# A transformer block on one Trainium2 core: the first batch's row maxima turned by quarters of the heads, the second's by halves

## The reference

```python
c6 = silu(c) @ Wc + bc            # six modulation vectors for each batch
sh_msa, sc_msa, g_msa, sh_mlp, sc_mlp, g_mlp = split(c6, 6)
xm = layernorm(x) * (1 + sc_msa) + sh_msa
q, k, v = (xm @ W + b).reshape(B, S, NH, DH)  for W, b in (q, k, v)
w = softmax((q / DH) @ k.T)                   # 512 x 512 for each batch and head
x = x + g_msa * ((w @ v) @ Wo + bo)
xm2 = layernorm(x) * (1 + sc_mlp) + sh_mlp
x = x + g_mlp * (gelu(xm2 @ W1 + b1) @ W2 + b2)
```

## Time and profile before

| | |
|---|---|
| Median of 3 runs | 773.78 us (772.47 to 776.5) |
| Profiled execution | 772.2 us |
| Its span in the profile | 770.0 us |
| Mean granted TensorE clock | 0.954 |
| PE busy | 709.4 us (92%) |
| DVE busy | 580.5 us (75%) |
| ACT busy | 391.1 us (51%) |
| POOL busy | 216.5 us (28%) |

### The profile page before, as it was taken

One profiled execution on the slowest core, in us unless ns is written; L12 is line 12 of the kernel. 1 busy time (PEld: TensorE's weight loads), 2 busy tenths in 40 slices (PEclk: granted clock), 3 DMA queues, 4 the chain that ended last, 5 costly groups with the idle time before them and its releaser, 6 DMA issues.

```text
span 770.0 us, 11786 instructions
## 1 busy us (share of the span) xinstructions
PE 709.4 (92%) x3967; PEld 382.9 (50%) x3967; DVE 580.5 (75%) x1019; ACT 391.1 (51%) x463; POOL 216.5 (28%) x162
## 2 busy tenths in 40 slices
PE   4788989869999999999999999999999998998996
PEld 2451222432378325762478225862478225822886
DVE  4779788959896998789886798789886986721563
ACT  5420556127742775257642675257633773298221
POOL 1454020200343032512162032412162022330444
PEclk9875899869999999999999999999999999999999
DMA  8599000771058303850076303840076102021110
GB/s 295 197 262 261 22 29 20 253 170 55 29 194 207 112 15 114 252 147 29 28 239 160 102 14 131 239 143 29 29 239 166 65 27 72 3 83 44 57 35 27
DMA packets 59846, 88.45 MB, mean 115 GB/s; under 512 B 6246, under 2 KB 47740, under 8 KB 56716
## 3 DMA queue, kind: packets, MB, share of 16 engines
q1 hardware_dynamic: 59788, 87.69, 37.0%
HBM read 49.35 MB, written 38.06 MB: 114 GB/s over the span
## 4 chain that ended last, share of the span: by engine, by line
PE 35%; issue 34%; DVE 14%; POOL 11%; ACT 3%; DMA 3%; POOLq 0%; SPq 0%; ACTq 0%; DVEq 0%
DVE mx L947 7%; PE ps L651 7%; PE ps L629 7%; PE ps L574 6%; PE ps L659 5%; POOL hl L462 4%; PE ps L795 4%; PE ps L799 2%; POOL prob L452 2%; ACT prob L520 2%; DVE prob L1019 1%; POOL x L432 1%; POOL xd L445 1%; PE ps L611 1%; PE ps L731 1%
## 5 line engine op out<-in xcount | busy, mean ns | idle before, releaser
L947 DVE TENSOR_REDUCE mx<-ps 128x1 f32<-128x512 f32 x512 | 336.0, 686 | 60.8 <-PE ps L629 54.7
L520 ACT ACTIVATE prob<-ps 128x1024 f32<-128x1024 f32 x256 | 247.8, 1022 | 155.4 <-PE ps L659 155.2
L629 PE MATMUL ps<-kst,qst 96*128 96x512 bf16 x512 | 197.5, 407 | 22.5 <-DVE mx L947 17.1
L659 PE MATMUL ps<-qst,kst 98*128 98x512 bf16 x512 | 150.6, 386 | 4.2 <-DMA qst<-mrow 2.7
L629 PEld LDWEIGHTS ps<-kst,qst 96*128 96x128 bf16 x512 | 45.5, 98 | 189.8 <-DVE mx L947 165.9
L651 PE MATMUL ps<-prob,vaug 128*32 128x512 f32 x1024 | 137.8, 610 | 0.5 <-ACT prob L520 0.3
L462 POOL TENSOR_TENSOR hl<-z,hh 128x512 fp32r<-128x512 f32 x64 | 82.3, 1286 | 136.5 <-DVE hh L1079 136.5
L561 ACT ACTIVATE z<-ps,bias_t 128x512 f32<-128x512 f32 x64 | 44.0, 688 | 134.7 <-PE ps L799 129.9
L409 POOL TENSOR_TENSOR rstd<-vare,mhalf 128x4 f32<-128x4 f32 x16 | 16.7, 1046 | 255.2 <-DVE vare L875 255.2
L659 PEld LDWEIGHTS ps<-qst,kst 98*128 98x128 bf16 x512 | 47.1, 99 | 70.6 <-ACT prob L520 26.9
L452 POOL TENSOR_TENSOR prob<-prob 128x512 bf16<-128x512 f32 x32 | 38.3, 1196 | 139.8 <-DVE prob L1022 139.8
(11 more groups left out here) (106 smaller groups left out, 833.0 us busy)
## 6 DMA issues: line engine op xcount, KB each, us to landing
parts_scratch<-prob SPq DMA_DIRECT2D x32, 384.0 KB, 2.9
qst<-parts_scratch SPq DMA_DIRECT2D x16, 768.0 KB, 9.1
kst<-parts_scratch SPq DMA_DIRECT2D x16, 768.0 KB, 13.6
parts_scratch<-prob SPq DMA_DIRECT2D x32, 256.0 KB, 3.2
y_scratch<-rb SPq DMA_DIRECT2D x32, 256.0 KB, 2.0
xa<-in_x_dram SPq DMA_DIRECT2D x8, 512.0 KB, 4.3
parts_scratch<-prob SPq DMA_DIRECT2D x32, 128.0 KB, 2.9
xd<-in_x_dram SPq DMA_DIRECT2D x8, 512.0 KB, 3.5
```

The source lines that it names most:

```text
L520: act.activation(prob[:, s % 2, 2 * p:2 * p + 2, :], ps[:, 2 * p:2 * p + 2, :], ACT.Exp, scale=1.0 / DH).then_inc(exp_done, 1)
L629: pe.matmul(ps[:, banks[n % len(banks)], :], qst[1 - par][0:MROW, h, t * P:(t + 1) * P], kst[1 - par][0:MROW, h, :], start=True, stop=True ...
L659: m = pe.matmul(ps[:, q, :], kst[par][0:KROWS, G * g + q, kt * P:(kt + 1) * P], qst[par][0:KROWS, G * g + q, :], start=True, stop=True)
L947: dve.tensor_reduce(mx[:, t, h:h + 1], ps[:, banks[n % len(banks)], :], AXX, ALU.max).then_inc(max_done, 1)
```

## The change

Four things are changed.

**Smaller turns.** Batch 0 is turned in four quarters: 18 blocks, the turn of heads 0 to 3, and 6 blocks in step -1; the other 40 in the first ten stages of C(0), with turns at s = 2, 6 and 10. Batch 1 is turned in two halves: 24 blocks in s = 10 to 15 of C(0), 6 in A, 2 behind it, the turn, 12 more; the other 20 in the first six stages of C(1), with a turn at s = 6. So the 64 blocks of batch 2 begin at s = 7 of step 1. From step 2 on the order of blocks is as before.

**The second batch's x** is loaded among the first loads, into `x1`; its statistics wait for that, and its normalisation and the splitting of Wv and Wo stand at another place in VectorE's order.

**Part writes.** Each part has one place in SBUF and is written by one transfer to all its slots, as soon as that part is there. There are as many transfers and bytes as before.

**Waits.** C(0) no longer waits for the low parts of the MLP weights on GpSimd (`const_set`); the products with Wo do.

```diff
-C_BLOCKS = (1, 0) + (3,) * (STEPS - 4) + (4, 4)
-TURN_BLOCKS, QK_BLOCKS, V_BLOCKS = (1, 1), (0, 1, 0, 1), (0, 1, 0, 1)
-UP_BLOCKS, DOWN_BLOCKS = (1, 1, 1), (2, 2, 2, 2, 2, 0, 0, 0)
-HALF, EXTRA = NH * TT // 2, 8
-OLD_BLOCKS = (4,) * 6 + (0,) * (STEPS - 6)
-NEW_BLOCKS = (0,) * 6 + (4,) * (STEPS - 6)
+QUARTER, HALF, EXTRA, SECOND = NH * TT // 4, NH * TT // 2, 8, 44
+Blocks = namedtuple("Blocks", "old new turn qk v up down")
+STEADY = Blocks((0,) * STEPS, (1, 0) + (3,) * (STEPS - 4) + (4, 4), (1, 1), (0, 1, 0, 1), (0, 1, 0, 1), (1, 1, 1), (2, 2, 2, 2, 2, 0, 0, 0))
+FIRST = Blocks((4,) * 10 + (0,) * 6, (0,) * 10 + (4,) * 6, (1, 1), (0, 1, 0, 1), (0, 1, 0, 1), (), ())
+NEXT = Blocks((2, 2, 4, 4, 4, 4) + (0,) * 10, (0,) * 7 + (3, 3) + (4,) * 7, (1, 1), (1,) * 4, (1,) * 4, (2, 2, 2), (3, 3, 3, 3, 2, 0, 0, 0))
+FIRST_TURNS, NEXT_TURNS = {2: 4, 6: 8, 10: 12}, {6: 8}
...
+            sp.dma_start(x1[:], x[1].rearrange("(t p) f -> p t f", p=P)).then_inc(xb_loaded, 16)
...
                 def write_parts(b, j):
-                    sp.wait_ge(part_l, 4 * b + j + 1)
-                    for slot, part, n in SLOT_RUNS[j // 2]:
-                        sp.dma_start(parts_scr[j, slot:slot + n].rearrange("n p s -> p n s"), parts[:, j, part:part + n, :])\
-                            .then_inc(parts_written[j], 16)
+                    for part, ready in enumerate((part_h, part_m, part_l)):
+                        at, step, n = PART_SLOTS[j // 2][part]
+                        sp.wait_ge(ready, 4 * b + j + 1)
+                        sp.dma_start(parts_scr[j, at:at + (n - 1) * step + 1:step].rearrange("n p s -> p n s"),
+                                     parts[:, j, part, :].unsqueeze(1).broadcast_to([P, n, S])).then_inc(parts_written[j], 16)
...
-                        pe.wait_ge(const_set, 6)
+                        pe.wait_ge(const_set, 3)
...
-                        if s == STEPS // 2 and not later(i, 0, 1):
-                            pe.wait_ge(m_loaded, 32)
+                        if s in (4, 8, 12) and at(i, 0) or s == 8 and at(i, 1):
+                            pe.wait_ge(m_loaded, 32 * turn_no(i, s))
...
+                        if turn is not None:
+                            turn_maxima(i, turn)
                         if s:
                             pv(i, par, s - 1)
-                        between(2, old + new)
-                        if s == OLD_TURN and not later(i, 0, 1):
-                            turn_maxima(i - 1, NH // 2, NH)
+                        between(2 if turn is None else 0, old + new)
...
                 elif early(i):
-                    scores(i, par, HALF + 2, (6, 7, 0, 1))
-                    turn_maxima(i, 0, NH // 2, half_turned, 4)
+                    scores(i, par, QUARTER + 2, (6, 7, 0, 1))
+                    turn_maxima(i + 1, 0, 4)
                     scores(i, par, EXTRA - 2)
                 else:
-                    scores(i, par, tail_blocks(i))
-                    turn_maxima(i)
+                    scores(i, par, HALF - block_at[0])
+                    turn_maxima(i + 1, 0)
+                    scores(i, par, SECOND - HALF)
```

More of the change, by code:

```diff
@@ L238, in x1_of, with at, blocks, c_turns @@
             return xa if final(b) else x1
[L240 to L247, removed]
+        def at(b, n):
+            return isinstance(b, int) and b == n
+        def blocks(i):
+            return FIRST if at(i, 0) else NEXT if at(i, 1) else STEADY
+        def c_turns(i):
+            return FIRST_TURNS if at(i, 0) else NEXT_TURNS if at(i, 1) else {}
+        def heads_of(b, head):
+            return head + (NH // 4 if at(b, 0) else NH // 2 if at(b, 1) else NH)
+        def turn_no(b, head):
+            return head // 4 + 1 if at(b, 0) else head // 8 + 5 if at(b, 1) else b + 5
         def early(i):
@@ L290, in step @@
             def step(i, par):
-                if runs(i, 2) and later(i, 2, 1) and not early(i) or early(i) and not later(i, 2, 1):
-                    b = i + 3 if early(i) else i + 2
+                if runs(i, 2) and not early(i):
+                    b = i + 2
                     sp.wait_ge(tp_done[0], b)
@@ L303, in step, with load_maxima @@
                     sp.dma_start(gm[:], c6_scr[bass.ds(i - 1, 1), G2 * H:(G2 + 1) * H].broadcast_to([P, H])).then_inc(gm_loaded, 16)
-                def load_maxima(stack, first, last, loaded):
+                def load_maxima(b, stack, head):
+                    last = heads_of(b, head)
+                    sp.wait_ge(mrow_done, 2 * turn_no(b, head))
                     for n in range(2):
-                        sp.dma_start(stack[MROW + n:MROW + n + 1, first:last, :], mrow[0:last - first, n, :]).then_inc(loaded, 16)
-                if runs(i, 0) and not later(i, 0, 1):
-                    sp.wait_ge(mrow_done, 2)
-                    load_maxima(qst[par], NH // 2, NH, m_loaded)
+                        sp.dma_start(stack[MROW + n:MROW + n + 1, head:last, :], mrow[0:last - head, n, :]).then_inc(m_loaded, 16)
                 if runs(i, 0):
+                    if at(i, 0):
+                        load_maxima(i, qst[par], 4)
                     for g in range(NG):
@@ L684, in step @@
                     for s in range(STEPS):
-                        old, new = c_blocks(i, s)
+                        old, new, turn = blocks(i).old[s], blocks(i).new[s], c_turns(i).get(s)
                         def between(first, last):
@@ L755, in step @@
                 else:
-                    scores(i, par, others(sum(QK_BLOCKS + V_BLOCKS)))
+                    scores(i, par, others(sum(blocks(i).qk + blocks(i).v)))
                 def wo_products(bank):
@@ L993, in step @@
                                     norm_piece(0, i + 2, xa, k)
-                    if s == OLD_TURN and has_c and not later(i, 0, 1):
-                        maxima_rows(i - 1, NH // 2)
-                row_max(i, others(TURN_BLOCKS[0]))
+                row_max(i, others(blocks(i).turn[0]))
                 if has_a:
@@ L1024, in step @@
                 for j in range(4):
+                    if j == 2 and has_a and not later(i, 2, 1):
+                        split_weights(1)
+                        for t in range(TT):
+                            normalise(0, 1, x1, t)
                     if j == 3:
-                        row_max(i, others(QK_BLOCKS[3] + sum(V_BLOCKS[0:2])))
+                        row_max(i, others(blocks(i).qk[3] + sum(blocks(i).v[0:2])))
                     if has_a:
```

148 lines of the change are left out of this document (76 added, 72 removed).

## The result

| | before | after |
|---|---|---|
| Median | 774.41 us (772.47 to 776.5, 4 runs) | 787.57 us (785.5 to 788.57, 4 runs) |
| Profiled execution, its span | 772.2, 770.0 us | 785.5, 783.7 us |

The changed kernel is slower: ratio 1.0154, 95% interval 1.0124 to 1.0184. The two spans differ by 13.7 us. Places in the program are read from one profiled execution of each kernel.

A forecast was written before the change was run, and what follows sets the result against it. TensorE (92% busy) and VectorE (75%) were taken to bound the kernel by where each waits. Terms -9.6 + 5.2 + 1.0 + 9.2 + 3.8 + 3.9 = +13.5 us gave 785.7, or 787 by median; predicted 786, range 774 to 792.

The forecast's parts named there:

- start of C(0): Step -1: 16 fewer blocks and an earlier start, but row loads wait behind the load of `qst`; -9.6 us.
- C(0): Same 64 blocks, but three turns at 2.5 us each and 0.6 for statistics, where one cost 2.86; +5.2 us.
- end of step 0: Before C(1): work 1.8 us shorter but worth nothing, because C(1) starts with the stack loads; 0 us.
- first product with v of C(1): Start of C(1): half clock 1.0 us, and blocks ahead waiting for VectorE to write x1, 2.85 us; +3.85 us.
- rest of C(1): C(1) after its first product with v: fuller stages, a turn, a row wait and layernorm pieces; +6.35 us.
- A of step 1: A, up to the MLP's first cast: five more blocks on a full VectorE; +3.8 us (2 to 4.5).
- MLP of step 1: Four times three blocks instead of two, each third waiting for VectorE; +3.9 us (1 to 5).
- the rival that they don't: Step -1: first rows don't wait behind the load of `qst`, C(0) starts at 62.2; 783 us, no separate chance.
- third rival: C(0): a quarter's rows come late, 1 to 2 us in three places; 790 us; late rows or slower clock 0.10.
- the fourth: C(0): turns are cheap and it begins at full clock, -3.2 and -1.6 us; 781 us, no separate chance.
- The wait at s = 8: C(1): rows of the turn at s = 6 land after they are needed; 0.9 us of waiting.
- rivals in which step 1 takes its blocks for nothing or by half: Step 1: blocks free, 769 us (free or nearly so 0.11), or half absorbed, 777 us (774 to 781: 0.17).

The follow-up runs named there:

- experiment 3: Changed kernel with the row loads of step -1 issued ahead of all four stack loads; ratio 1.0124 to the kernel before.
- Experiment 8: Changed kernel with the row loads of steps -1 and 0 issued by ScalarE instead of SyncE; ratio 1.0133 to the kernel before.
- experiment 4: Changed kernel with the row loads of step 0 issued ahead of the four stack loads of step 0; ratio 1.0095 to the kernel before.
- experiment 5: Changed kernel with one block instead of four ahead of C(1)'s first product with v, three more ending step 0; ratio 1.0118 to the kernel before.
- experiment 6: Changed kernel with the third block in step 1's MLP issued behind the next up products, not ahead; ratio 1.0131 to the kernel before.
- experiment 7: Changed kernel with batch 0 in quarters but batch 1 not split, its 34 remaining blocks ending step 0; ratio 1.0019 to the kernel before.
- experiment 10: Changed kernel with rows first in steps -1 and 0, one block ahead of C(1)'s first product with v, third MLP blocks later; ratio 0.9991 to before.
- 11: Kernel before with both start edits and step 0's row loads between the stack loads of heads 0 to 7 and 8 to 15; ratio 0.9891, median 768.06 us.
- 1: Kernel before with the start edits alone: batch 1's x among the first loads, each part written by one transfer; ratio 0.9952 to before.
- 9: Kernel before with step 0's row loads placed between the stack loads of heads 0 to 7 and 8 to 15; ratio 0.9954 to before.

## Why the prediction was right

Sign and time (786 against 787.57 us) held, and so did the steps in kind, but their sizes less well. The sum is 0.3 us off between the two profiles because misses of up to 1.3 us with both signs cancel; that closeness is luck. By the points of the sum, against the profiled execution:

| Step | predicted | measured | from |
|---|---|---|---|
| start of C(0) | -9.6 | -9.17 | 74.97 to 65.80 |
| C(0) | +5.2 | +4.29 | last product with v 131.54 to 126.66 |
| end of step 0 | 0 | +0.07 | start of C(1) 167.85 to 163.04 |
| first product with v of C(1) | +3.85 | +4.35 | 171.25 to 170.79 |
| rest of C(1) | +6.35 | +5.19 | 210.65 to 215.38 |
| A of step 1 | +3.8 | +5.09 | 229.15 to 238.97 |
| MLP of step 1 | +3.9 | +3.94 | 246.98 to 260.74 |
| sum | +13.5 | +13.8 | |

*Start.* Modulation at 34.84 us, forecast 34.5; the first row maximum 2.5 us earlier, forecast 2.6. *Step -1.* The rows did wait: from the second copy's end (59.85) to C(0) it took 5.95 us, against 3.27 where nothing large stands ahead; the rival that they don't falls by the chain, and experiment 3 shows what it would have given. I wrote that they wait behind the load of `qst`; they landed 0.2 us from the 65.3 us that I had worked out for it. Experiment 8 shows that their queue is not the reason. *C(0).* A turn cost 2.2 us on average, not 2.5: that term was mis-sized. The late quarters of the third rival didn't come: no wait for rows at s = 4, 8 and 12. Nor did the full clock of the fourth: it was 0.50 from 65 to 75 us.

*End of step 0.* Worth nothing, as said, because C(1) starts with the transfers; experiment 4 shows this from the other side. The half clock cost about 1 us: the Wo products with the low part took 2.27 us instead of 1.30. *C(1).* The four blocks ahead of the first product with v cost what was said, and experiment 5 gives 3.4 us of it back. The wait at s = 8 was 0.16 us, not 0.9: that term was mis-sized, since the load came 2.6 us after its issue and not 3.3 us after the copies.

*A of step 1* is the term that was too small, 3.8 against 5.1, above my upper bound of 4.5. I counted each block's own maximum. I counted neither the 2.54 us cast that stands between two of them nor what a wait does to the clock. The cast and a wait behind it were there before too (2.58 and 1.50 us); with more blocks around it the waits became 0.69 and 2.72 us, 1.9 us more. Behind the second the granted clock was 0.62, and blocks took 0.65 us instead of 0.39: three groups of one block and six products took 4.40 us (229.00 to 233.40), where one such group took 0.94 before (220.82 to 221.76), so 1.6 us are the clock. The seven blocks added up to there are TensorE's own work, 1.5 us as an estimate from 0.22 for one in A and 0.21 for one behind the up products (1.84 us apart instead of 1.63). That makes 5.0 of the 5.09 us; without the clock it would have been near 3.5. *MLP.* Right in size and in cause (experiment 6).

The rivals in which step 1 takes its blocks for nothing or by half fall: experiment 7, without the split of batch 1, is 1.35% faster. That a split with all waits repaired comes out at 0.9991 (experiment 10), while the two edits that don't touch the turns give 0.9891 (11), says where the change went wrong. It took 20 blocks from the end of step 0. That brought the start of C(1) from 173.32 us (experiment 7) to 163.04, 10.3 us, less than the 12 to 14 us that 20 blocks take there (0.60 to 0.69 us each), since C(1) then waited for its rows. And it put them where they cost 18.6 us, by the table's rows from the first product with v of C(1) to the MLP: 0.52 us for one in C(1) (3.14 us a stage instead of 2.62), 0.95 us in the MLP (4.22 instead of 3.27), with a turn and the waits on top. No run splits batch 1 and leaves batch 0 in halves. That the ratios gain more than the profiled spans in experiments 1, 9 and 11 fits the profile of before, which is 4 us under its median; the profiles of 1 and 9 are 0.3 and 1.6 us under theirs, and that of 11 is 1.1 us above. Which places of the program differ between executions of one kernel stays open.

## What to carry to other kernels

A small transfer that a whole engine waits for should be issued ahead of large ones. Another queue did not help here while the large ones were under way, and holding back the stack loads that were needed last cost nothing. Work that is moved off a serial stretch must go where both engines of its hand-over have room at that moment: in the MLP VectorE had room on average, and still each third block waited for it, until other work of TensorE was put ahead (experiment 6). Each extra synchronisation is paid on top. When a start is moved forward, look for the next wait that is tied to something else, for there the gain may end. And a wait of one engine for another can cost more than itself, if the clock falls behind it.

## What the hardware showed that I had not expected

The cast of 128x512 f32 to bf16 on VectorE takes 0.43 us, and 2.54 us where GpSimd has begun a 128x1024 f32 subtraction 0.1 us earlier (225.71 and 225.81 us above); both end within 0.3 us of each other. It is in the kernel before as well:

```profile
220.80 2.38 POOL L413 TENSOR_TENSOR zl<-z,zh 128x1024 fp32r<-128x1024 f32 x1
220.89 2.58 DVE L1022 CAST prob<-prob 128x512 bf16<-128x512 f32 x1
```

The Trainium skill's "SBUF — State Buffer", "SBUF: two separate sides", describes a port pair that VectorE and GpSimd hold in turn, for a whole instruction. The pairs of rows fit, and so does the same cast in step 0, where no such subtraction stands beside it: 0.43 us at 136.61 after and at 141.48 before. So does a shorter one: at 218.76 before, a cast took 0.83 us that had begun under a GpSimd subtraction of 1.17 us (from 218.14), and it ended 0.28 us behind that. No run moved the subtraction away from the cast, so the cause is argued from these rows, not shown by an experiment.

The row loads show how much a small transfer can cost. In step -1, 4 KB took 7.65 us with four loads of 768 KB issued before them, 4.87 us with two, and under 3 us with none (experiment 3). The count alone doesn't set it, for it matters how much of the loads is still under way. In step 0, rows issued right behind all four took 14.79 us in the changed kernel (148.21 to 163.00), and 7.61 us in the kernel before, where they were issued some 7 us behind the last of the four.
